# Attention logits straight from the normalised input, and a new order for every engine

## The reference

```
x = x + 0.5 * ffn(layernorm(x))
x = x + attn(layernorm(x))
x = x + 0.5 * ffn(layernorm(x))

ffn(x):   h = silu(x @ W1.T * s1) * (x @ W2.T * s2)        # 128 -> 512, weights in {-1, 0, 1}
          h = gelu(h @ H1.T * sh1);  h = gelu(h @ H2.T * sh2)   # 512 -> 512, twice
          return h @ W3.T * s3                              # 512 -> 128
attn(x):  h = layer_norm(x) * gamma + beta
          keys = h @ Wk.T + bk;  values = h @ Wv.T + bv
          key_att = keys @ Wka.T + bka
          w = exp(key_att / sqrt(128));  w = w / cumsum(w)  # along the sequence
          return cumsum(w * keys) * values
```

## Time and profile before

| | us |
|---|---|
| median of 3 runs (lowest, highest) | 390.57 (389.44, 391.17) |
| the profiled execution | 389.6 |
| its span in the profile | 387.8 |
| PE busy in the span | 378.7 (98%) |
| DVE busy | 335.1 (86%) |
| ACT busy | 305.2 (79%) |
| POOL busy | 48.2 (12%) |

### The profile page before, as it was taken

The page is one execution under the profiler, slowest core; times in us unless marked ns, Lnnn a source line. Parts: engine busy times, 40 slices in busy tenths (PEclk is TensorE's granted clock), DMA queues, the critical chain, the costliest instruction groups (busy, mean ns, idle before and its releaser), DMA issues.

```text
span 387.8 us, 5921 instructions
## 1 busy us (share of the span) xinstructions
PE 378.7 (98%) x1686; PEld 293.6 (76%) x1686; DVE 335.1 (86%) x755; ACT 305.2 (79%) x517; POOL 48.2 (12%) x70
## 2 busy tenths in 40 slices
PE   7999999999999999999999999999999999999996
PEld 2577888787777877777688787777877777788884
DVE  4898778899899998998999899799989989976733
ACT  3888778987786899689689967968898778686762
POOL 3821101110100311010022010100211010020000
PEclk9999999999999999999999999999999999999999
DMA  7700000000000000000000000000000000000001
GB/s 245 282 11 1 0 2 1 0 3 0 1 2 0 0 0 0 0 0 0 0 0 0 0 0 27 0 0 27 0 0 27 0 27 0 27 2 1 27 2 56
DMA packets 4045, 7.45 MB, mean 19 GB/s; under 512 B 576, under 2 KB 1472, under 8 KB 3904
## 3 DMA queue, kind: packets, MB, share of 16 engines
q1 hardware_dynamic: 3312, 6.36, 4.6%
q10 hardware_dynamic: 720, 0.93, 0.7%
HBM read 5.19 MB, written 2.10 MB: 19 GB/s over the span
## 4 chain that ended last, share of the span: by engine, by line
PE 77%; DVE 12%; issue 5%; ACT 4%; DMA 1%; POOL 0%; DVEq 0%; ACTq 0%
PE hid_ps L425 51%; PE gate_ps L425 6%; PE up_ps L425 5%; PE y_ps L425 5%; DVE rcsum L920 3%; PE y_ps L438 2%; PE xt_ps L438 2%; PE xt_ps L593 2%; DVE full L835 1%; DVE csum L915 1%; ACT L750 1%; DVE gate L825 1%; ACT full L675 1%; PE xt_ps L596 1%; PE xt_ps L599 1%
## 5 line engine op out<-in xcount | busy, mean ns | idle before, releaser
L425 PE MATMUL hid_ps<-act_hi,hi_h 128*128 128x512 f32 x496 | 202.3, 408 | 0.0
L425 PE MATMUL hid_ps<-act_lo,hi_h 128*128 128x512 f32 x496 | 193.4, 390 | 0.5 <-DVE act_lo L845 0.5
L845 DVE TENSOR_TENSOR act_lo<-full,act_hi 128x512 fp32r<-128x512 f32 x184 | 120.8, 683 | 24.0 <-ACT act_hi L680 18.2
L675 ACT ACTIVATE full<-hid_ps,vec 128x512 f32<-128x512 f32 x127 | 87.2, 686 | 40.5 <-PE hid_ps L425 36.7
L425 PEld LDWEIGHTS hid_ps<-act_lo,hi_h 128*128 128x128 f32 x496 | 93.2, 188 | 23.4 <-issue 4.1
L425 PEld LDWEIGHTS hid_ps<-act_hi,hi_h 128*128 128x128 f32 x496 | 93.2, 188 | 23.0 <-issue 4.1
L680 ACT ACTIVATE act_hi<-full 128x512 fp32r<-128x512 f32 x127 | 78.6, 628 | 4.2 <-POOL nmr L321 2.8
L319 POOL TENSOR_TENSOR rstd<-veps,half 128x4 f32<-128x4 f32 x24 | 29.6, 1234 | 291.1 <-DVE veps L805 291.1
L835 DVE SCALAR_TENSOR_TENSOR full<-up_ps,s_half,gate 128x512 f32<-128x512 f32 x63 | 46.8, 743 | 1.3
L658 ACT ACTIVATE tanh<-gate_ps,s_half 128x512 f32<-128x512 f32 x63 | 42.3, 682 | 6.1 <-PE gate_ps L425 5.1
L825 DVE SCALAR_TENSOR_TENSOR gate<-tanh,gate_ps 128x512 f32<-128x512 f32 x63 | 42.8, 679 | 0.4 <-ACT tanh L658 0.2
(11 more groups left out here) (124 smaller groups left out, 381.3 us busy)
## 6 DMA issues: line engine op xcount, KB each, us to landing
out<-x_sb SPq DMA_DIRECT2D x7, 256.0 KB, 2.0
x_sb<-x SPq DMA_DIRECT2D x1, 1536.0 KB, 6.4
raw_h<-h2t SPq DMA_DIRECT2D x4, 256.0 KB, 7.6
raw_h<-h1t SPq DMA_DIRECT2D x2, 256.0 KB, 6.5
raw_h<-h1t ACTq DMA_DIRECT2D x2, 256.0 KB, 7.1
raw_w<-w1t SPq DMA_DIRECT2D x1, 256.0 KB, 4.0
raw_w<-w2t ACTq DMA_DIRECT2D x1, 256.0 KB, 4.3
x_sb<-x SPq DMA_DIRECT2D x1, 256.0 KB, 6.5
```

Of the source, the lines that this page charges most:

```text
L425: mm = eng.matmul(ps, w, a, start=(first and n == 0), stop=(last and n == len(seq_) - 1))
L675: eng.activation(full23[m % 2][:, :], hid_ps[m % 2][:, :], ACT.Gelu, scale=col("sh1" if n == 2 else "sh2", m)).then_inc(s_gelu[n], 1)
L845: eng.tensor_tensor(act_lo[a][:, m, :], full[m % 2][:, :], act_hi[a][:, m, :].bitcast(F32), ALU.subtract).then_inc(s_lo[n], 1)
```

## The change

Since keys = Wk h + bk, the logits are Wka keys + bka = (Wka Wk) h + (Wka bk + bka). The changed kernel multiplies Wka and Wk once on the chip (`0:fold` in the first step, with a fourth load of Wk in its untransposed form), copies the product to `wl` on DVE and makes the logits' bias `bka_s` from the second, one-column matmul. In each attention tile the logits matmul then reads `wl` and `h_t` and can stand ahead of the keys' matmul. Exp now waits for `weight` of the tile before, and `weight_keys` for `keys`. All rows of FIRST_STEP and ORDER are written anew for PE, ACT and DVE; START and LAST_STEP stay.

```
-            for dst, src in ((wk, wkt), (wka, wkat), (wv, wvt)):
+            for dst, src in ((wk, wkt), (wka, wkat), (wv, wvt), (wk_rows, wkn)):
...
+                    elif stage == "fold":
+                        free("xt", (s_folded, 2))
+                        eng.wait_ge(s_watt, 64)
+                        eng.matmul(xt_ps[:, 0:D], wk_rows[:, :], wka[:, :], start=True, stop=True)
+                        eng.matmul(xt_ps[:, D:D + 1], wka[:, :], col("bk"), start=True, stop=True).then_inc(s_fold, 1)
                     elif stage == "att_keys":
                         free("xt", (s_keysb, t + 1))
-                        eng.wait_ge(s_watt, 48)
                         eng.matmul(xt_ps[:, :], wk[:, :], h_t[:, :], start=True, stop=True).then_inc(s_key, 1)
                     elif stage == "att_logits":
                         free("xt", (s_kw, t + 1))
-                        eng.matmul(xt_ps[:, :], wka[:, :], keys[:, :], start=True, stop=True).then_inc(s_att, 1)
+                        eng.matmul(xt_ps[:, :], wl[:, :], h_t[:, :], start=True, stop=True).then_inc(s_att, 1)
...
+            def fold():
+                eng.wait_ge(s_fold, 1)
+                eng.tensor_copy(wl[:, :], xt_ps[:, 0:D]).then_inc(s_folded, 1)
+                eng.tensor_scalar(bka_s[:, :], xt_ps[:, D:D + 1], col("bka"), SCALE, ALU.add,
+                                  ALU.mult).then_inc(s_folded, 1)
...
 FIRST_STEP = {
-    "PE": "p1.3 p3.0 p3.1 p3.2 p3.3",
+    "PE": "0:fold p1.3 p3.0 p3.1 p3.2 p3.3",
-    "DVE": "bits:h2.2 bits:h2.3 bits:w3 low2.0 flag:raise2 gate.0 up.0 low2.1 flag:copy2 low1.0 gate.1 up.1 "
+    "DVE": "bits:w3 bits:h2.2 stats bits:h2.3 aggr gate.0 up.0 flag:raise2 low2.0 gate.1 veps flag:copy2 up.1 "
...
```

PE's rows in the loop, before and after (one line for each step):

```
-        "p2.0 p2.1 t p2.2 p1.0 p1.1 p2.3 a:t p1.2 p4 p1.3 a:keys p3.0 p3.1 dt a:logits p3.2 p3.3",
+        "p2.0 p2.1 t p2.2 p1.0 p1.1 p2.3 a:t p1.2 p4 a:logits p1.3 p3.0 dt a:keys p3.1 p3.2 p3.3",
-        "t p2.0 p2.1 p1.0 p1.1 p4 p2.2 a:values p2.3 b:t dt p1.2 p1.3 a:dt p3.0 b:keys p3.1 p3.2 p3.3 "
-        "b:logits",
+        "p2.0 t p2.1 p2.2 p1.0 p1.1 a:values p4 p2.3 dt b:t p1.2 a:dt b:logits p1.3 p3.0 b:keys p3.1 p3.2 p3.3",
-        "p4 p2.0 p2.1 t p2.2 p1.0 dt b:values p1.1 p2.3 p1.2 b:dt p3.0 p1.3 p3.1 p3.2 p3.3",
+        "p2.0 p2.1 p4 t p2.2 p1.0 p1.1 b:values dt p2.3 p1.2 b:dt p3.0 p3.1 p1.3 p3.2 p3.3",
```

More of the change, by code:

```diff
@@ L39 @@
         "stats aggr veps bits:w1 norm",
-        "bits:w2 t vec:scales bits:h1.0 stats gate.0 up.0 aggr veps gate.1 flag:raise1 up.1 flag:copy1 "
-        "gate.2 up.2 gate.3 up.3 low1.3 1:t",
+        "bits:w2 t vec:scales bits:h1.0 stats gate.0 up.0 aggr veps gate.1 flag:raise1 up.1 flag:copy1 gate.2 up.2 "
+        "gate.3 up.3 low1.3 1:t",
     ),
@@ L47 @@
 FIRST_STEP = {
-    "PE": "p1.3 p3.0 p3.1 p3.2 p3.3",
-    "ACT": "bits:h2.0 gelu2.0 high2.0 bits:h2.1 tanh.0 gelu2.1 high2.1 tanh.1 high1.0 gelu2.2 high2.2 high1.1 gelu2.3 "
-           "tanh.2 high2.3 tanh.3 high1.2 gelu3.0 high3.0 high1.3 gelu3.1 high3.1 gelu3.2 high3.2 zwait z gelu3.3 "
-           "high3.3",
-    "DVE": "bits:h2.2 bits:h2.3 bits:w3 low2.0 flag:raise2 gate.0 up.0 low2.1 flag:copy2 low1.0 gate.1 up.1 "
-           "low2.2 low1.1 stats gate.2 low2.3 up.2 gate.3 aggr veps up.3 low1.2 low3.0 low1.3 low3.1 norm low3.2 low3.3",
+    "PE": "0:fold p1.3 p3.0 p3.1 p3.2 p3.3",
+    "ACT": "bits:h2.1 bits:h2.0 gelu2.0 tanh.0 high2.0 gelu2.1 tanh.1 high2.1 gelu2.2 high1.0 high2.2 high1.1 "
+           "gelu2.3 tanh.2 high2.3 gelu3.0 tanh.3 high1.2 high3.0 zwait gelu3.1 z gelu3.2 high3.1 high1.3 high3.2 "
+           "gelu3.3 high3.3",
+    "DVE": "bits:w3 bits:h2.2 stats bits:h2.3 aggr gate.0 up.0 flag:raise2 low2.0 gate.1 veps flag:copy2 up.1 "
+           "low2.1 low1.0 low2.2 gate.2 low2.3 up.2 low1.1 gate.3 low1.2 low3.0 up.3 low3.1 low1.3 0:fold low3.2 "
+           "low3.3 norm",
 }
@@ L65 @@
[L65 to L75, removed]
[10 rows of a table added]
     ),
     "DVE": (
-        "a:stats a:aggr a:veps t low2.0 a:norm stats low2.1 gate.0 up.0 aggr veps gate.1 low2.2 up.1 gate.2 "
-        "low1.0 up.2 low2.3 low1.1 gate.3 up.3 low1.2 norm dt low3.0 low1.3 b:stats a:cumsum b:aggr b:veps "
@@ L80 @@
[L80 to L85, removed]
@@ L86 @@
-        "low3.2 low3.3",
-        "stats t low2.0 aggr low2.1 gate.0 veps up.0 low2.2 low2.3 gate.1 norm up.1 low1.0 low1.1 gate.2 "
-        "up.2 low3.0 gate.3 up.3 low1.2 low3.1 low1.3 dt low3.2 low3.3",
[10 rows of a table added]
     ),
@@ L94 @@
           "last:dt.0 last:dt.1",
-    "ACT": "gelu2.0 gelu2.1 high2.0 high2.1 gelu2.2 high2.2 gelu2.3 high2.3 gelu3.0 p4 high3.0 gelu3.1 high3.1 gelu3.2 "
-           "high3.2 last:gelu.0 last:gelu.1 last:delta",
+    "ACT": "gelu2.0 gelu2.1 high2.0 high2.1 gelu2.2 high2.2 gelu2.3 high2.3 gelu3.0 p4 high3.0 gelu3.1 high3.1 "
+           "gelu3.2 high3.2 last:gelu.0 last:gelu.1 last:delta",
     "DVE": "low2.0 low2.1 low2.2 low2.3 low3.0 low3.1 dt low3.2 last:delta last:dt.0 last:dt.1",
@@ L103, with macaron_block @@
          "up": 1, "high1": 1, "low1": 1, "p4": -1, "dt": -1}
-def macaron_block(nc, x, w1t, w2t, h1t, h2t, w3t, wkt, wkat, wvt, vecs, out, seq):
+def macaron_block(nc, x, w1t, w2t, h1t, h2t, w3t, wkt, wkat, wvt, wkn, vecs, out, seq):
     D = wkt.shape[0]
@@ L305, in _ @@
         def _(eng):
-            for s in (s_adelta, s_x2, s_wgk, s_za):
+            for s in (s_adelta, s_x2, s_wg, s_wgk, s_za):
                 eng.sem_inc(s, 1)
@@ L860, in emit @@
                     scales()
+                elif stage == "fold":
+                    fold()
                 elif stage == "stats":
```

15 lines of the change are left out of this document (9 added, 6 removed), and 21 rows, old and new, of the table ORDER.

## The result

The changed kernel takes 384.26 us (383.79 to 384.59, four runs) against 390.7 (389.44 to 391.17, four runs): 0.9839 of the time before, with a 95% interval of 0.9813 to 0.9865. A second series gave 384.28 against 390.76, 0.9834 (0.9820 to 0.9848). The forecast said 386.6 with a range that began at 384.6. The profiled execution took 384.05, its span is 382.0, 5.8 less than before.

What follows compares the result with a forecast made beforehand. PE, busy 378.7 of 387.8 us, was taken as the bound. From the profiled 389.6, 4 x (1.2 - 0.2) = 4.0 for the loop and 0.0 for the first step gave 385.6, plus 1.0 to the median 386.6; range 384.6 to 390.4.

Steps and rivals of the forecast that it cites:

- The old waits: Four places per loop iteration where PE's matmuls stand too far apart: 1.16 us together, taken as 1.2.
- A: Start of loop step 1: the matmul after the transposes waits 0.15 us for a bank released by a gelu.
- B: Start of loop step 2: p4 wants the last low3, a wait of 0.18 us per iteration.
- C: First p1 of loop step 2: xn_lo starts late, behind two reciprocals on DVE, 0.59 us per iteration.
- D: Attention transposes in loop step 2: they wait for adelta, 0.24 us per iteration.
- The new waits: Loop stalls the new order would bring as DVE's work is pulled forward: 0.2 us per iteration.
- The first step: Ahead of the loop: -0.83 for low2.3, +0.53 for the flag, +0.3 for the fold, 0.0 us in sum.
- The flag: In the first step, the flag's matmul waits because raise2 moves later on DVE: a loss of 0.53 us.
- low2.3's wait: Before the loop, PE's wait of 0.96 us for low2.3, which would go: a gain of 0.83 us.
- The shorter chain is worth nothing by itself: Rival for the loop: the order alone does the work; same time as the forecast, no chance of its own.
- One wait for another: Rival: step 2's first group waits for low1.2 and low1.3, a stall of 0.7 to 0.8; 389.0 us, chance 0.20.
- All of it goes: Rival: no new stall in the loop, and the first step's gain of 0.8 stays; 385.0 us, chance 0.14.

Runs made afterwards that it cites:

- e8: The changed kernel with the loop's reciprocals left out and tanh in place of Exp, nothing moved: 383.73 us, ratio 0.9833 to the kernel before.
- e15: The changed kernel itself, unaltered, measured again in a second series: 384.28 us, ratio 0.9834 to the kernel before.
- e1: The kernel before with only the new attention arithmetic (fold, logits from wl and h_t, Exp's new wait), all orders as before: 391.1 us, ratio 1.0009.
- e2: The kernel before with the new arithmetic and the new first step, the loop's orders as before: 390.39 us, ratio 1.0001.
- e7: The kernel before with aggr and veps of the loop's third step moved ahead of gate.3 on DVE: 389.88 us against 390.04, ratio 0.9993.
- e5: The kernel before with the four reciprocals of a pass left out, nothing moved: 389.44 us, ratio 0.9979.
- e4: The changed kernel's orders with the old arithmetic, keys and logits exchanged, cumulative sums and reciprocals re-placed on DVE: 409.16 us, ratio 1.0476 to the kernel before.
- e9: The new arithmetic in the orders of before, with logits and Exp exchanged with keys, tile b's logits also ahead of p3.0: 394.66 us, ratio 1.0119.
- e13: The changed kernel with p4 put back to the head of the third step on PE: 400.85 us, ratio 1.0253 to the kernel before.
- e14: The changed kernel with tile b's values (adelta) moved back on DVE behind low2.2, dt, gate.1 and up.1: 386.01 us, ratio 0.9879 to the kernel before.
- e3: The changed kernel with the first step of before and the fold in it: 384.25 us, ratio 0.9838 to the kernel before.
- e10: The kernel before with tile b's values (adelta) moved on DVE to right behind pool, ahead of dt, up.0 and gate.1: 391.58 us, ratio 1.0042.
- e11: New arithmetic in the orders of before with early Exp, early adelta of tile b, and veps ahead of gate.3: 396.48 us, ratio 1.0172.
- e6: The kernel before with tanh in place of Exp, so the loop's table loads fall away, nothing moved: 386.96 us, ratio 0.9922.

## Why the forecast was right or wrong

The measured 384.26 lies 2.3 below the forecast. 1.55 of that is in the profiled execution, where 385.6 was forecast and 384.05 measured, and 0.8 in the step from there to the median.

*What bounds it: right.* PE's waits were all there was to win in the loop, and all of it was won.

*The old waits, "1.16 per iteration, I say 1.2": too small.* By distances between starts, before minus after, A is 0.18, B 0.19, C 0.60, D 0.30 and the second p1 of step 2 0.09 (0.32 between its first two starts, now 0.23); some 0.1 is in pieces of 0.01 or 0.02. That is 1.47. "The other 0.8 of an iteration is spread in pieces under 0.1, and I leave it": 0.3 of it were waits, the rest is PE's own pace (e8). The forecast gave 70.1 to 70.4 as the sign of being right, which the 69.88 is not; its own test for this error, a period under 69.8, was missed by 0.08, and the conclusion holds all the same. 4 x 0.27 = 1.1.

*The new waits, "I take 0.2 per iteration": this term failed.* It measured 0.0 (e8: 6.1 us less DVE work changes nothing). No margin failed, not those of 0.15 and 0.3 either, and the two that were measured by using them up are as laid out. I had worked each place out without a wait and then added one for doubt. 4 x 0.2 = 0.8. Both terms make a pass of 70.35 where 69.88 was measured, 1.9 in all. The first step gave 0.2 more than forecast. The other way went 0.3 behind PE's last instruction (4.00 before, 4.28 after, and 3.72 in e15, so it is no part of the change) and 0.25 around the span (384.05 - 382.0 against 1.8). So the profiled execution came out at 384.05 where 385.6 was forecast.

*From the profiled execution to the median: an addition that didn't stay.* I added 1.0, since before's median lies that far above its profiled execution. After it is 0.2. In e1 and e2, which keep before's orders in the loop, passes of 71.4 change with passes of 71.8, where POOL's rstd takes 2.58; the one execution of before that was profiled has none of those. In the changed kernel rstd takes 2.58 too, but what waits for it has the time, and every pass is 69.9. That before's other executions have such passes fits this and is not shown; e7, which takes the wait away alone, was too near to before to tell.

*The first step: near in sum.* The flag cost 0.29 where 0.53 was forecast, the fold 0.37 and low2.3's wait went, -0.83 + 0.29 + 0.37 = -0.2; by before, e1 and e2 it is worth 0.2.

*C "behind two reciprocals": half of it.* xn_hi on ACT was late too, to within 0.2 (e5). Both hang on Exp, so the step as made took both away, but with the reciprocals alone gone 0.39 of C's 0.60 stayed.

*"The shorter chain is worth nothing by itself": right, and not the whole story.* By itself it brings nothing (e1), and without it the new orders lose 4.8% in the one layout that was tried (e4). An early Exp in the old order loses 1.2% (e9). The gain is in neither part by itself. Of the single moves that were taken back, p4's and adelta's places in step 2 are needed (e13, e14), the new first step hardly (e3).

*"One wait for another"* did not happen here, but it is what three smaller changes met (e9, e10, e11), at 0.6 to 0.8 a place. *"All of it goes"*, 385.0, came nearest, and for the loop it was right: no new wait. That its number is only 0.7 off is partly luck, since it took the old waits for 1.1 too little and the first step for 0.6 too much.

## What to carry to other kernels

Where the busiest engine stands at 98% and a second one at 94%, a wait that you take away by moving one stage or a few can come back one group later: three such moves lost time here (e9, e10, e11), and the order that was laid out as a whole, with every buffer's reader at its place, kept the gain. Leaving work out is another matter (e6 gained 3.1 us with nothing moved). An operand can be late for two reasons that end at nearly the same time: ask of each wait what would be late next, on the other engine too, before you price it. When a layout has been worked out place by place and no wait is in it, put the doubt into the range and not into the likeliest value; and when you carry a profiled execution over to a median, look first what makes the runs differ.
